# Second norm of the local layers on token rows between two turns, with a new order of the work

## The chip, the cores and the metric

One core of a Trainium2 chip (of eight) runs the whole program. The metric is the device time of one execution in microseconds (us). Engines: PE is TensorE (PEld its weight loads), DVE VectorE, ACT ScalarE, POOL GpSimd, SP SyncE, whose queue carries the transfers.

## The reference

x has the shape (8, 1024, 128), float32. Everything lies between two macaron halves and a causal attention of one head:

```python
x = x + 0.5 * local(layernorm(x))          # 2 layers of local attention and a gated second half
x = x + attention(layernorm(x), Wk, Wq, Wv)
x = x + 0.5 * local(layernorm(x))
# one layer of local(): 8 heads of 64, windows of 64 tokens that look one window back
h = shift_token(x); q, k, v = split(h @ wqkv)
q, k = rotary(l2norm(q) * qs, l2norm(k) * ks)
x = x + softmax(mask(8 * q @ k.T)) @ v @ wo
h = shift_token(x)
h = (h - mean(h)) / sqrt(var(h) + 1e-5) * ln_g + ln_b      # the second norm, over 128 features
a, g = split(h @ w1 + b1)                                  # 2 x 341
x = x + (a * gelu(g)) @ w2 + b2
```

## The kernel before, in words

x stays in SBUF as token rows. The state of a local layer, Y0, lies features on partitions and tokens along them, one row of 1026 columns per batch. 8192 tokens make 32 chunks of 256 (`NCH`). One chunk in one layer is a turn t: turns 0 to 63 are the two layers of the first half, 64 to 127 those of the second. Two turns are a pair u, for which the second half of the layer runs on 512 tokens. Layers 0 and 2 (the "even" ones) make their input from x by a first norm: `ln_stats`, `ln_root`, `ln_scale`, `ln_rows`, `turn_ln`, `y0_up`, `y0_down`. Layers 1 and 3 ("odd") turn their output back (`turn_y`) and add it to x (`x_next`).

A turn has two halves i of 128 tokens: `project` (three passes of fp32r, high and low parts), `square`, `sum_squares`, `rotate_cos`, `rotate_sin`, `rotate_add`, the twelve small steps of `root` (reciprocal root of the heads' norms by bit trick and three refinements), `normalise_qk`, `turn`, copies, `scores`, `row_max`, `exp_rows`, `row_inverse`, `scale_p`, `turn_p`, `copy_p`, `values`, `split_o`, `rest_of_o`, `wo`. A pair then has `y1_low` and `y1_high` (residual added, second token shift made), and the second norm. It runs with features on partitions: `split_yc` (ACT) and `rest_of_yc` (POOL) split Y1 into high and low fp32r parts NH and NL; `center` (PE, L656, L657) multiplies both by I - 1/128; `square_c` (ACT, L3680) squares; `var` (PE, L678) sums the squares over features by four products with a column of 1/128, tokens now on partitions; `add_eps` (DVE, L1955); `row_rstd` (POOL, L4725) takes the power -0.5; `turn_rstd` (PE, L686) spreads the four columns over all features by transposes; `copy_rstd` (ACT); `normalise` (DVE, L1963); `split_hn` (ACT) and `rest_of_hn` (POOL) split again. Then `to_gate`, `gelu`, `to_up`, `gate`, `down` (L710) and `y_next`.

Each engine follows a list of steps written out by hand: `first_steps`, `local(phase)` as a loop over rounds s (two turns and one pair per round, with fixed lags), `into_attention`, `attention`, `out_of_attention`, `last_steps`. Waits are on semaphores of the step's own inputs. PSUM has eight banks; `ROTA` and `FIRST_USERS` fix which steps use a bank in which order, and `vacant` lets a step wait until the bank's user before it has been read out:

```python
before = BEFORE[what, n]
if before:
    for done in emptied[before[0]]:
        on.wait_ge(done, emptied_at(*before))
```

Of the kernel before, what the change touches and what calls it, by code (L numbers as in the profile page):

```python
# [5335 lines left out]
```

## Time and profile before

| | |
|---|---|
| runs | 2748.17, 2749.38 (median), 2749.87 us |
| the profiled execution | 2748.73 us, of which its span 2746.9 us |
| PE busy | 2663.2 us (97%) |
| PEld busy | 2122.3 us (77%) |
| DVE busy | 2372.5 us (86%) |
| ACT busy | 2373.0 us (86%) |
| POOL busy | 2114.2 us (77%) |
| mean granted clock of TensorE | 0.993 |
| share of PE in the chain that ended last | 87% |

The span runs from the first to the last instruction; the rest of the time lies around it. Busy times are unions of an engine's instructions; PE's matmuls overlap, so that a share near 100% of the span can hold pipelining. "PS" is PSUM. A 128x128 fp32 matmul or 512-wide fp32 product counts as two instructions of the trace where it runs in two passes.

### The profile page before, as it was taken

To read this page: it belongs to the slowest core of one execution; us is meant where nothing else is said; L and a number is where in the kernel's file an instruction comes from. 1 tells how busy PE (TensorE), PEld (TensorE's weight loads), DVE (VectorE), ACT (ScalarE), POOL (GpSimd) and SP (SyncE) were. 2 spreads that over 40 slices of the span, in tenths; PEclk is the share of its full clock that TensorE was granted. 3 is DMA by queue.
4 is the path that set the end of the run, shared out by engine and by line. 5 is a ranking of instruction groups with operands and counts; after the bars stand their busy time and mean duration, and the time that the engine had idled before them with its cause. 6 is when DMAs were issued, how large, how long until landed. Compare 5 with 4: busy or idle time off the path is not lost.

```text
span 2746.9 us, 80395 instructions
## 1 busy us (share of the span) xinstructions
PE 2663.2 (97%) x29432; PEld 2122.3 (77%) x29432; DVE 2372.5 (86%) x6140; ACT 2373.0 (86%) x7281; POOL 2114.2 (77%) x2121
## 2 busy tenths in 40 slices
PE   5999999999999999999999999999999999999998
PEld 3777777778788888886777777787778788888886
DVE  7998999988888888896778999999998888888884
ACT  4998999999999999996443999999999999999995
POOL 6888888889888888882102988888889888888883
PEclk9999999999999999999999999999999999999998
DMA  3111111111111111110000111111111111111111
GB/s 96 46 44 30 27 38 23 31 27 34 31 23 31 31 37 28 31 23 12 8 1 3 35 27 29 30 33 31 23 31 30 30 31 34 36 38 31 38 31 32
DMA packets 63811, 83.96 MB, mean 31 GB/s; under 512 B 11539, under 2 KB 30653, under 8 KB 63421
## 3 DMA queue, kind: packets, MB, share of 16 engines
q1 hardware_dynamic: 63420, 78.82, 12.5%
q8 instruction: 238, 3.90, 0.6%
q14 instruction: 153, 1.25, 0.2%
HBM read 11.67 MB, written 4.19 MB: 6 GB/s over the span
## 4 chain that ended last, share of the span: by engine, by line
PE 87%; DVE 7%; issue 3%; ACT 1%; POOL 1%; DMA 0%; SPq 0%; POOLq 0%; DVEq 0%; ACTq 0%
PE PS L633 9%; PE PS L617 8%; PE PS L583 8%; PE PS L607 8%; PE PS L574 7%; PE PS L576 6%; PE PS L710 6%; PE PS L575 6%; PE PS L691 3%; PE PS L599 3%; PE PS L693 2%; PE PS L692 2%; PE PS L775 2%; PE PS L678 2%; PE PS L647 2%
## 5 line engine op out<-in xcount | busy, mean ns | idle before, releaser
L3652 ACT ACTIVATE P<-PS,MX 128x128 f32<-128x128 f32 x2048 | 735.2, 402 | 31.9 <-DVE MX L1912 31.0
L4714 POOL TENSOR_TENSOR P<-P,RI 128x512 f32<-128x512 f32 x512 | 532.0, 1043 | 226.3 <-DVE RI L1918 226.2
L4678 POOL TENSOR_TENSOR T<-T,SQ 128x512 f32<-128x512 f32 x512 | 654.5, 1287 | 55.7 <-DVE SQ L1877 32.8
L4691 POOL TENSOR_TENSOR T<-T,RN 128x512 f32<-128x512 f32 x512 | 527.8, 1048 | 33.2 <-DVE RN L1906 32.9
L3652 ACT ACTIVATION_READ_ACCUMULATOR P<-PS,MX 128x1 f32 x2048 | 489.9, 240 | 0.0
L574 PE MATMUL PS<-WH,YH 128*128 128x512 f32 x768 | 365.5, 476 | 30.1 <-DVE RV L1955 13.9
L3607 ACT ACTIVATE SQ<-PS 128x512 f32<-128x512 f32 x512 | 334.9, 656 | 63.9 <-PE PS L576 39.5
L1869 DVE TENSOR_TENSOR T<-PS,TAB 128x512 f32<-128x512 f32 x512 | 347.8, 681 | 37.4 <-ACT SQ L3607 35.1
L3659 ACT COPY PT<-PS 128x512 f32<-128x512 f32 x512 | 317.7, 631 | 52.3 <-PE PS L617 47.6
L1912 DVE TENSOR_REDUCE MX<-PS 128x4 f32<-128x512 f32 x512 | 347.4, 681 | 11.0 <-PE PS L607 6.5
L1877 DVE TENSOR_TENSOR SQ<-PS,TAB 128x512 f32<-128x512 f32 x512 | 348.4, 682 | 4.1
L1858 DVE TENSOR_REDUCE SS<-SQ 128x8 f32<-128x512 f32 x512 | 335.7, 674 | 5.2 <-ACT SQ L3607 4.2
L617 PE MATMUL PS<-CST,P 128*128 128x128 f32 x2048 | 313.9, 277 | 0.2 <-POOL P L4714 0.2
L633 PEld LDWEIGHTS PS<-PT,VP 128*64 128x64 f32 x8192 | 259.0, 138 | 65.2 <-issue 64.7
L576 PE MATMUL PS<-WH,YL 128*128 128x512 f32 x768 | 307.2, 400 | 0.0
L575 PE MATMUL PS<-WL,YH 128*128 128x512 f32 x768 | 305.4, 398 | 0.0
L583 PE MATMUL PS<-CST,T 128*128 128x128 f32 x2048 | 292.1, 276 | 6.6 <-POOL T L4691 4.0
L633 PE MATMUL PS<-PT,VP 128*64 128x64 f32 x8192 | 293.2, 225 | 1.3 <-ACT PT L3659 1.1
L583 PEld LDWEIGHTS PS<-CST,T 128*128 128x128 f32 x2048 | 237.0, 141 | 47.5 <-issue 18.1
L607 PE MATMUL PS<-KT,QT 64*64 64x128 f32 x8192 | 268.6, 270 | 0.0
L617 PEld LDWEIGHTS PS<-CST,P 128*128 128x128 f32 x2048 | 237.1, 141 | 31.1 <-issue 4.0
L607 PEld LDWEIGHTS PS<-KT,QT 64*64 64x64 f32 x8192 | 242.7, 133 | 17.9 <-issue 0.2
(135 smaller groups left out, 6085.5 us busy)
## 6 DMA issues: line engine op xcount, KB each, us to landing
VP<-VP SPq DMA_DIRECT2D x480, 128.0 KB, 2.3
out_dram<-X SPq DMA_DIRECT2D x16, 256.0 KB, 2.6
X<-in_L_attn_x_dram SPq DMA_DIRECT2D x7, 512.0 KB, 4.5
SG<-in_L_ffn_w_dram SPq DMA_DIRECT2D x5, 341.0 KB, 2.9
SG<-in_L_ffn_wqkv_dram SPq DMA_DIRECT2D x4, 384.0 KB, 3.4
SGQ<-in_L_ffn_wqkv_dram SPq DMA_DIRECT2D x4, 256.0 KB, 3.5
X<-in_table_dram SPq DMA_DIRECT2D x2, 512.0 KB, 6.1
P<-in_L_ffn_wo_dram SPq DMA_DIRECT2D x2, 256.0 KB, 3.1
```

The lines of the kernel that those rows point to most:

```text
L574: pe.matmul(PS[:, b, :], YH[:, k, :], WH[:, cols], start=True, stop=False)
L575: pe.matmul(PS[:, b, :], YH[:, k, :], WL[:, cols], start=False, stop=False)
L576: pe.matmul(PS[:, b, :], YL[:, k, :], WH[:, cols], start=False, stop=True).then_inc(projected[x], 1)
L583: ins = pe.transpose(PS[:, b, 128 * p:128 * p + 128], T1[:, k, 128 * p:128 * p + 128], ident)
L607: ins = pe.matmul(PS[64 * w:64 * w + 64, bank_of(f"S{2 * i + x}", t), 128 * p:128 * p + 128], QT2[at, s, p, m:m + WIN], KT[at, p, k:k + 12 ...
L617: ins = pe.transpose(PS[:, b, 128 * p:128 * p + 128], P[:, g, p, :], ident)
L633: ins = pe.matmul(PS[64 * x:64 * x + 64, b, 128 * p + m:128 * p + m + WIN], VP[:, s, 2 * i + w, d:d + 64], PT[:, 2 * i + x, p, m:m + WIN], ...
L1877: dve.tensor_tensor(SQ[:, (2 * n + 1 - x) % 3, :].rearrange("p (h t d) -> p h t d", h=HEADS, t=2), PS[:, b, :].rearrange("p (h t d) -> p h ...
L3652: ins = act.activation(P[:, g, p, :], PS[:, b, 128 * p:128 * p + 128], ACT.Exp, bias=MX[:, g, p:p + 1], accum_out=SM[:, g, p:p + 1])
L4678: pool.tensor_tensor(T1[:, k, :], T1[:, k, :], SQ[:, (2 * n + 1 - x) % 3, :], ALU.add).then_inc(added[x], 1)
L4691: pool.tensor_tensor(heads, heads, RN[:, t % 2, i, 8 * x:8 * x + 8].unsqueeze(2).broadcast_to([128, HEADS, DH]), ALU.mult).then_inc(scaled ...
L4714: pool.tensor_tensor(P[:, g], P[:, g], RI[:, g, :].unsqueeze(2).broadcast_to([128, NPAIR, 128]), ALU.mult).then_inc(p_scaled, 1)
```

## The change

The second norm goes over to token rows. `turn_rows` (PE) turns the four 128x128 blocks of Y1 into PSUM; `rows_stats` (DVE) takes mean and variance of each token by BN_STATS and BN_AGGR from there, adds eps and negates the means; `row_rstd` (POOL) takes the power and multiplies it with the negated means; `norm_rows` (ACT) applies scale and bias to the four blocks; `turn_back` (PE) turns them back; `split_hn` (ACT) reads PSUM, times ln_g, into NH, and `rest_of_hn` (DVE) forms NL. `center`, `var`, `turn_rstd`, `square_c`, `copy_rstd`, `add_eps`, `normalise`, `split_yc` and `rest_of_yc` go. The b1 products move from the variance bank into the bank of two `turn_ln` steps (turns 0 and 1), and the split of W1 (`round_w1`, `rest_of_w1`) becomes a step of its own. The lists of all engines and the users of all banks are new.

```diff
-OF_PAIRS = ("WO", "CE", "VA", "RS", "G0", "G1", "G2", "W2", "YT")
-ROUNDS = {0: (6, 32), 1: (38, 62)}
+OF_PAIRS = ("WO", "YR", "HB", "G0", "G1", "G2", "W2", "YT")
+ROUNDS = {0: (8, 32), 1: (40, 62)}
...
+    [("LT", 7), ("TK1", 9), ("YR", 6), ("P0", 9), ("HB", 6), ("P2", 9), ("LT", 6), ("G1", 6)],
...
-        def center(u):
...
-            pe.matmul(PS[:, b, :], CEN[:], NH[:], start=True, stop=False)
-            pe.matmul(PS[:, b, :], CEN[:], NL[:], start=False, stop=True).then_inc(center_mm, 1)
...
+        def turn_rows(u):
+            b, m = bank_of("YR", u), within(u)
+            on.wait_ge(y1_done, 2 * u + 2)
+            vacant(on, "YR", u)
+            for i in range(2 * TPC):
+                ins = pe.transpose(PS[:, b, 128 * i:128 * i + 128], Y1[:, m + 128 * i:m + 128 * i + 128], ident)
+            ins.then_inc(rows_turned, 1)
...
-            for i in range(2 * TPC):
-                ins = pe.matmul(PS[:, b, i:i + 1], SQL[:, 128 * i:128 * i + 128], ones, start=True, stop=True)
-            ins.then_inc(var_mm, 1)
...
-        def turn_rstd(u):
+        def turn_back(u):
+            b = bank_of("HB", u)
+            vacant(on, "HB", u)
+            on.wait_ge(rows_normed, u + 1)
             for i in range(2 * TPC):
+                ins = pe.transpose(PS[:, b, 128 * i:128 * i + 128], RN_ROWS[:, 128 * i:128 * i + 128], ident)
+            ins.then_inc(back_turned, 1)
...
+        def rows_stats(u):
+            b, n = bank_of("YR", u), 2 * TPC
+            done = (2 * n + 2) * u
+            on.wait_ge(rows_turned, u + 1)
+            on.wait_ge(rows_normed, u)
+            for i in range(n):
+                dve.bn_stats(RST[:, i, :], PS[:, b, 128 * i:128 * i + 128]).then_inc(row_stat, 1)
+            for i in range(n):
+                on.wait_ge(row_stat, done + i + 1)
+                dve.bn_aggr(RMV[:, i, :], RST[:, i, :]).then_inc(row_stat, 1)
+            on.wait_ge(row_stat, done + 2 * n)
+            dve.tensor_scalar(RMV[:, :, 1], RMV[:, :, 1], EPS, None, ALU.add).then_inc(row_stat, 1)
+            dve.tensor_scalar(RNM[:], RMV[:, :, 0], -1.0, None, ALU.mult).then_inc(row_stat, 1)
+
+        def rest_of_hn(u):
+            gamma = COLS[:, layer_of_pair(u) % 2, 6:7]
...
+            dve.scalar_tensor_tensor(NL[:], PS[:, bank_of("HB", u), :], gamma, NH[:].bitcast(F32), ALU.mult,
+                                     ALU.subtract).then_inc(hn_lo, 1)
...
+        def norm_rows(u):
+            b = bank_of("YR", u)
...
+            on.wait_ge(rstd, u + 1)
+            on.wait_ge(row_biased, u + 1)
+            for i in range(2 * TPC):
+                ins = act.activation(RN_ROWS[:, 128 * i:128 * i + 128], PS[:, b, 128 * i:128 * i + 128], ACT.Identity,
+                                     bias=RSB[:, 1, i:i + 1], scale=RSB[:, 0, i:i + 1])
+            ins.then_inc(rows_normed, 1)
...
+        def split_hn(u):
...
+            act.activation(NH[:], PS[:, bank_of("HB", u), :], ACT.Identity,
+                           scale=COLS[:, layer_of_pair(u) % 2, 6:7]).then_inc(hn_hi, 1)
...
         def row_rstd(u):
...
+            pool.tensor_tensor(RSB[:, 0, :], RMV[:, :, 1], NHALF[:], ALU.pow).then_inc(rstd, 1)
+            on.wait_ge(rstd, u + 1)
+            pool.tensor_tensor(RSB[:, 1, :], RSB[:, 0, :], RNM[:], ALU.mult).then_inc(row_biased, 1)
```

Where the steps stand now is shown at three places. First TensorE in a round of the kernel before, from the end of turn_p through centring (L656, L657), values (L633), scores (L599, L607) and the variance products (L678):

```order
L617 MATMUL PS<-CST,P 128x128 x4
L656 MATMUL PS<-NH,CEN 128x512
L657 MATMUL PS<-NL,CEN 128x512
L574 MATMUL PS<-WH,YH 128x512
L575 MATMUL PS<-WL,YH 128x512
L576 MATMUL PS<-WH,YL 128x512
L633 MATMUL PS<-PT,VP 64x64 x16
L599 MATMUL PS<-MLOC,IDB 64x512 x4
L607 MATMUL PS<-KT,QT 64x128 x16
L678 MATMUL PS<-CST,G 128x1 x4
```

Nothing but these and turn_rstd, a little later, belongs to the norm on TensorE. In the changed kernel the same engine, in an odd layer, has turn_rows (L682) ahead of both values (L659), turn_y (L746), projections (L600 to L602) and scores (L625, L633), up to the next turn_p (L643):

```order
L643 MATMUL PS<-CST,P 128x128 x4
L682 MATMUL PS<-CST,Y 128x128 x4
L659 MATMUL PS<-PT,VP 64x64 x32
L746 MATMUL PS<-CST,G 128x128 x4
L600 MATMUL PS<-WH,YH 128x512
L601 MATMUL PS<-WL,YH 128x512
L602 MATMUL PS<-WH,YL 128x512
L625 MATMUL PS<-MLOC,IDB 64x512 x4
L633 MATMUL PS<-KT,QT 64x128 x16
L600 MATMUL PS<-WH,YH 128x512
L601 MATMUL PS<-WL,YH 128x512
L602 MATMUL PS<-WH,YL 128x512
```

One more projection follows, then the turn_p that uses the bank of the turned rows again; turn_back (L699) comes after two more projections and two turns. On VectorE of the changed kernel the statistics (L2148 to L2154) stand between two steps of the root (L2095, L2097), behind a row maximum (L2105) and the last sine product of the turn (L2070):

```order
L2089 TENSOR_SCALAR PS<-PS 128x32
L2105 TENSOR_REDUCE MX<-PS 128x4
L2093 TENSOR_SCALAR RN<-PS 128x32
L2070 TENSOR_TENSOR SQ<-PS,TAB 128x512
L2095 SCALAR_TENSOR_TENSOR PS<-RN,PS 128x32
L2148 BN_STATS RST<-PS 128x6 x4
L2151 BN_AGGR RMV<-RST 128x2 x4
L2153 TENSOR_SCALAR RMV<-RMV 128x4
L2154 TENSOR_SCALAR RNM<-RMV 128x4
L2097 TENSOR_TENSOR PS<-PS,RN 128x32
```

In the kernel before, only add_eps stood in such a place, one small instruction; now ten do. GpSimd's next step behind the rotate_add of that sine product is row_rstd.

## Rows read from the trace of the kernel before

**Rows 1.** Stretches: us; busy of PE, PEld, DVE, ACT, POOL; PEclk, DMA share, GB/s

```profile
325.69:481.14 155.45, 152.43 (x1754) 121.11 (x1753) 142.97 (x383) 143.87 (x447) 132.33 (x135) 1.00 0.14 32
...
861.26:1011.74 150.48, 150.20 (x1754) 121.54 (x1753) 131.18 (x313) 141.11 (x440) 126.97 (x127) 1.00 0.14 33
```

**Rows 2.** Chain that ended last, its longest pieces: start us, us, what

```profile
286.84 2.58 PE PS L710 x6
...
598.02 2.58 PE PS L710 x6
673.25 2.58 PE PS L710 x6
...
1199.72 2.58 PE PS L710 x6
```

**Rows 3.** The same chain within one odd round

```profile
872.74 0.23 PE PS L656
...
873.91 1.08 PE PS L633 x32
874.99 0.34 PE PS L599 x4
875.33 0.87 PE PS L607 x32
876.20 0.98 PE PS L678 x8
...
878.97 0.44 PE PS L686 x4
```

**Rows 4.** Waits in four even rounds, 325.69 to 481.14: us in total, times, longest

```profile
DVE Y L1847 <- PE PS L720: 5.0, 4, 1.3
...
DVE Y L1987 <- PE PS L710: 4.4, 4, 1.1
```

**Rows 5.** VectorE in order of time, even round: start us, us, engine, line, operation

```profile
382.58 0.47 DVE L1799 BATCH_NORM_STATS2 ST<-X 128x6 f32<-128x128 f32 x2
382.97 0.30 DVE L1802 BATCH_NORM_AGGREGATE MV<-ST 128x2 f32<-128x6 f32 x2
383.30 0.74 DVE L1804 TENSOR_SCALAR MV<-MV 128x2 f32<-128x2 f32 x1
383.96 0.23 DVE L1918 RECIPROCAL RI<-SM 128x4 f32<-128x4 f32 x2
...
387.38 0.17 DVE L1804 TENSOR_SCALAR MV<-MV 128x2 f32<-128x2 f32 x1
387.46 0.18 DVE L1918 RECIPROCAL RI<-SM 128x4 f32<-128x4 f32 x1
```

**Rows 6.** GpSimd in order of time, the same stretch

```profile
381.97 2.05 POOL L4691 TENSOR_TENSOR T<-T,RN 128x512 f32<-128x512 f32 x2
...
387.72 1.04 POOL L4714 TENSOR_TENSOR P<-P,RI 128x512 f32<-128x512 f32 x1 [0.47 <-DVE RI L1918]
```

**Rows 7.** ScalarE in order of time, odd round

```profile
873.30 0.60 ACT L3680 ACTIVATE G<-PS 128x512 f32<-128x512 f32 x1
873.80 0.36 ACT L3652 ACTIVATE P<-PS,MX 128x128 f32<-128x128 f32 x1
874.05 0.20 ACT L3652 ACTIVATION_READ_ACCUMULATOR P<-PS,MX 128x1 f32 x1
874.14 0.37 ACT L3652 ACTIVATE P<-PS,MX 128x128 f32<-128x128 f32 x1
```

**Rows 8.** The chain that ended last, in the tail

```profile
2706.22 1.12 PE PS L686 x4
...
2725.86 1.01 POOL RV L4725
2726.87 3.94 issue
...
2732.16 0.80 PE PS L691
```

More of the change, by code:

```diff
@@ new lines, in local @@
+                project(t - 8, 0, Q)
+                down(s - 7)
+                turn(t - 9, 1, K)
+                project(t - 8, 1, K)
+                turn_p(t - 10, 0)
+                turn_p(t - 10, 1)
+                turn_p(t - 10, 2)
+                project(t - 8, 1, Q)
+                scores(t - 9, 0)
+                turn(t - 9, 1, Q)
+                turn_p(t - 10, 3)
+                turn_rows(s - 6)
+                values(t - 10, 0)
+                values(t - 10, 1)
+                turn_y(s - 7)
@@ new lines, in local @@
+                project(t - 8, 0, V)
+                scores(t - 9, 1)
+                project(t - 7, 0, Q)
+                project(t - 8, 1, V)
+                turn_p(t - 9, 0)
+                project(t - 7, 0, K)
+                project(t - 7, 1, K)
+                turn(t - 8, 0, Q)
+                turn(t - 8, 0, K)
+                turn_back(s - 6)
+                project(t - 7, 1, Q)
+                scores(t - 8, 0)
+                turn_p(t - 9, 1)
+                turn(t - 8, 1, K)
@@ new lines, in first_steps @@
+            rotate_sin(9, 0, K)
+            rotate_cos(9, 0, K)
+            ln_stats(10)
+            row_inverse(7, 3)
+            row_max(8, 0)
+            sum_squares(9, 1, K)
+            rest_of_hn(2)
+            rotate_cos(9, 1, K)
+            rotate_sin(9, 1, K)
+            row_inverse(8, 0)
+            row_max(8, 1)
+            sum_squares(9, 1, Q)
+            rotate_cos(9, 1, Q)
+            root(9, 0)
+            ln_scale(10)
+            root(9, 1)
+            ln_rows(10)
@@ new lines, in first_steps @@
+            root(9, 2)
+            rotate_sin(9, 1, Q)
+            root(9, 3)
+            row_inverse(8, 1)
+            root(9, 4)
+            y0_up(10)
+            root(9, 5)
+            rest_of_o(7, 0)
+            root(9, 6)
+            rest_of_o(7, 1)
+            root(9, 7)
+            ln_stats(11)
+            root(9, 8)
+            row_max(8, 2)
+            root(9, 9)
+            gate(2, 0)
+            gate(2, 1)
+            root(9, 10)
+            root(9, 11)
+            ln_scale(11)
@@ new lines, in first_steps @@
+            row_max(8, 3)
+            gate(2, 2)
+            ln_rows(11)
+            y1_low(3)
+            row_inverse(8, 2)
+            sum_squares(10, 0, K)
+            y0_up(11)
+            y1_high(3)
+            row_inverse(8, 3)
+            rotate_cos(10, 0, K)
+            rotate_sin(10, 0, K)
+            sum_squares(10, 0, Q)
+            rotate_cos(10, 0, Q)
+            rotate_sin(10, 0, Q)
+            y_next(2)
+            sum_squares(10, 1, K)
+            rotate_cos(10, 1, K)
@@ new lines, in first_steps @@
+            sum_squares(11, 1, K)
+            rest_of_hn(3)
+            rotate_cos(11, 1, K)
+            rotate_sin(11, 1, K)
+            row_inverse(10, 0)
+            row_max(10, 1)
+            sum_squares(11, 1, Q)
+            rotate_cos(11, 1, Q)
+            root(11, 0)
+            ln_scale(12)
+            root(11, 1)
+            ln_rows(12)
+            root(11, 2)
+            rotate_sin(11, 1, Q)
+            root(11, 3)
+            row_inverse(10, 1)
+            root(11, 4)
@@ new lines, in first_steps @@
+            y0_up(12)
+            root(11, 5)
+            rest_of_o(9, 0)
+            root(11, 6)
+            rest_of_o(9, 1)
+            root(11, 7)
+            ln_stats(13)
+            root(11, 8)
+            row_max(10, 2)
+            root(11, 9)
+            gate(3, 0)
+            gate(3, 1)
+            root(11, 10)
+            root(11, 11)
+            ln_scale(13)
+            row_max(10, 3)
+            gate(3, 2)
+            ln_rows(13)
+            y1_low(4)
+            row_inverse(10, 2)
@@ new lines, in first_steps @@
+            sum_squares(12, 0, K)
+            y0_up(13)
+            y1_high(4)
+            row_inverse(10, 3)
+            rotate_cos(12, 0, K)
+            rotate_sin(12, 0, K)
+            sum_squares(12, 0, Q)
+            rotate_cos(12, 0, Q)
+            rotate_sin(12, 0, Q)
+            y_next(3)
+            sum_squares(12, 1, K)
+            rotate_cos(12, 1, K)
+            rotate_sin(12, 1, K)
+            sum_squares(12, 1, Q)
+            row_max(11, 0)
+            root(12, 0)
+            rotate_cos(12, 1, Q)
@@ new lines, in first_steps @@
+            row_max(12, 1)
+            sum_squares(13, 1, Q)
+            rotate_cos(13, 1, Q)
+            root(13, 0)
+            ln_scale(14)
+            root(13, 1)
+            ln_rows(14)
+            root(13, 2)
+            rotate_sin(13, 1, Q)
+            root(13, 3)
+            row_inverse(12, 1)
+            root(13, 4)
+            y0_up(14)
+            root(13, 5)
+            rest_of_o(11, 0)
+            root(13, 6)
+            rest_of_o(11, 1)
+            root(13, 7)
+            ln_stats(15)
@@ new lines, in first_steps @@
+            root(13, 8)
+            row_max(12, 2)
+            root(13, 9)
+            gate(4, 0)
+            gate(4, 1)
+            root(13, 10)
+            root(13, 11)
+            ln_scale(15)
+            row_max(12, 3)
+            gate(4, 2)
+            ln_rows(15)
+            y1_low(5)
+            row_inverse(12, 2)
+            sum_squares(14, 0, K)
+            y0_up(15)
+            y1_high(5)
+            row_inverse(12, 3)
+            rotate_cos(14, 0, K)
+            rotate_sin(14, 0, K)
@@ new lines, in first_steps @@
+            sum_squares(14, 0, Q)
+            rotate_cos(14, 0, Q)
+            rotate_sin(14, 0, Q)
+            y_next(4)
+            sum_squares(14, 1, K)
+            rotate_cos(14, 1, K)
+            rotate_sin(14, 1, K)
+            sum_squares(14, 1, Q)
+            row_max(13, 0)
+            root(14, 0)
+            rotate_cos(14, 1, Q)
+            root(14, 1)
+            row_max(13, 1)
+            root(14, 2)
+            rotate_sin(14, 1, Q)
+            root(14, 3)
+            rows_stats(5)
```

4682 lines of the change are left out of this document (2623 added, 2059 removed), and 234 rows, old and new, of tables (FIRST_USERS, LAST_USERS, ROTA).

## Prediction

> **What bounds the kernel now.** I read the stretches of time first, then the chain of waits, then the waits by engine, then single rows of the engines. A round is two turns of the local layers with one second half (one pair); 64 pairs are worked off. The rows of the down projection (L710), one per round, give the period. In layers that make their input by a first norm (even layers) eight rounds take 598.02 - 286.84 = 311.2 us, 38.90 each; in those that turn their output back (odd layers) fourteen rounds take 1199.72 - 673.25 = 526.5 us, 37.60 each [rows 2]. The stretches say what limits them: in four odd rounds of 37.62 us TensorE is busy for 150.20 of 150.48 us, at full clock, while VectorE has 131.18, ScalarE 141.11 and GpSimd 126.97. In four even rounds of 38.86 us TensorE has 152.43 of 155.45, VectorE 142.97 [rows 1]. Odd rounds are TensorE's. Even rounds belong to nobody: VectorE stands twice per round for TensorE, 5.0 us at y0_up and 4.4 us at y_next in four rounds [rows 4], and TensorE comes late in turn. Without these waits (9.4 / 4 = 2.35) VectorE needs 38.86 - 2.35 = 36.5 us of an even round. In an odd one it has 131.18 / 4 = 32.8 busy; with the same small gaps between its own instructions (36.5 - 142.97 / 4 = 0.8) it needs 33.6.
>
> **TensorE, per pair.** A busy sum overstates pipelined matmuls, so prices come from the chain, where one follows another [rows 3]. Removed: centring, two passes of 0.23 as at L656 = 0.46; the variance products, 0.98; the four transposes that spread the root, 0.44. Sum 1.88. Added: turn_rows and turn_back, four transposes each, priced as the four of L686: 2 x 0.44 = 0.88. Net -1.00. All of it lies in the path of odd rounds: 37.60 - 1.00 = 36.6. Bounds: 0.2 more is saved if what follows the variance products no longer starts late; 0.3 less if the new transposes stand behind 64-row matmuls, as some of today's do.
>
> **VectorE, per pair.** The token-row statistics stand in rows that exist today for the first norm [rows 5]: BATCH_NORM_STATS2, two from 382.58 to 382.97, 0.195 each; BATCH_NORM_AGGREGATE, two to 383.30, 0.165 each; TENSOR_SCALAR 0.08 (387.38 to 387.46). rows_stats is 4 x 0.195 + 4 x 0.165 + 2 x 0.08 = 1.60. It loses add_eps (0.08, same kind). The 512-wide normalise becomes the 512-wide rest_of_hn, both with one PSUM and one SBUF operand: nothing. Net +1.5. Reading PSUM instead of SBUF is seen in no row for these operations; I take 0 and keep +0.1 each.
> The first TENSOR_SCALAR of the same round costs 0.66 (383.30 to 383.96), and it ends as GpSimd ends its run of two operations at 384.02 [rows 5, 6]; the one at 387.38 falls into a gap of GpSimd and costs 0.08. So each of the two new small operations may cost 0.08 or up to some 0.66. In the new order they stand where GpSimd's next instruction is row_rstd, which waits for them, so I take 0.08. The Trainium skill (SBUF — State Buffer, "two physically separate sides") says that a VectorE operation in a two-port mode and a GpSimd operation exclude each other for the whole instruction. By that rule both would be dear whenever GpSimd is busy, and the sum would be some 1.2 us per pair higher; the pair of rows above agrees with it.
> New need of VectorE: odd 33.6 + 1.5 = 35.1, under TensorE's 36.6: hidden, with 1.5 us of cover. Even 36.5 + 1.5 = 38.0, over TensorE's: so **even rounds become VectorE's, at 38.0** if the new order takes away the two standing waits of 2.35. It is built for that: y_next, today at once behind a gate and a row maximum, gets eight operations of about 0.6 behind the last gate; y0_up gets about one us behind ln_rows. I count nothing for the steps of the reciprocal root standing less often directly behind each other, and keep -0.5 for it.
>
> **ScalarE and GpSimd.** ScalarE loses four 512-wide passes of 0.50 (873.30 to 873.80) = 2.0 and gets four 128-wide ones of 0.25 (873.80 to 874.05) and one of 0.50 [rows 7]: -0.5, from 141.11 / 4 = 35.3, so it stays under 36.6. Table loads stay two per round, since the new passes stand among the exponentials' operations and the three gelus stand together. GpSimd loses two 512-wide subtractions of 1.0 or more each (two operations in 2.05, rows 6) and gets one 128x4 product, at most the 1.01 of the power beside it [rows 8]. It only gets more room.
>
> **Waits that are added.** Bank 3 now holds in turn turn_rows, turn_p(.,0), turn_back, turn_p(.,2). turn_p(.,0) must wait until ScalarE has emptied the turned rows. TensorE has between them two times values (1.08), turn_y (0.44), three projections of three passes as wide as centring's (3 x 0.23 = 0.70 each) and scores (0.34 + 0.87): 2.16 + 0.44 + 2.10 + 1.21 = 5.9 us [rows 3]. The way round is rows_stats 1.6, power 1.0, product 0.1 to 1.0, norm_rows 1.0, and four handovers of about 0.1: 4.1 to 5.0. That leaves 0.9 to 1.8 us for VectorE's lag behind TensorE at that point (four 512-wide operations stand between the last thing it must wait for and rows_stats). turn_back waits for ScalarE's copy of turn_p(.,0), behind which stand a square, one group of exponentials (four times 873.80 to 874.14, 1.4) and another square: again about level. I count 0, with +0.5 per round as the upper end. Queued behind a late turn_p are the projections and all that follow.
>
> **Ends.** The last pair has nothing to hide behind. Its chain from the power on holds 3.94 us of issue and starts the gate products only at 2732.16, the first of them 0.80 long [rows 8]. New: before the power a turn (0.44) and 1.6 in place of cast, subtraction, centring, square and variance (about 0.5 + 1.0 + 0.46 + 0.5 + 0.98 = 3.4), and behind it a product of up to 1.0, 1.0, 0.44, 0.5 and 0.66 (3.6) in place of 5.3: together 3 us less. The first rounds, and the crossing into and out of the middle attention, hold four more pairs at half the gain. Moving the b1 products into the bank of the first norm's turn, and the rounding of W1, happens two and four times in all: nothing. SP's queue keeps its transfers.
>
> **Sum.** Odd rounds 33 x 1.0 = 33; even rounds 27 x (38.90 - 38.0) = 24; four mixed pairs 4 x 0.5 = 2; end 3. Total 62 us from the profiled execution's own 2748.7 us: 2686.7. The median shown is 0.65 above that execution: **2687 us**, -2.3%.
>
> **Rivals.**
> - B, VectorE never binds: root steps interleave better (-0.5) and even rounds, too, run at TensorE's pace plus a little, 37.2. For: VectorE's gaps are latency. Against: 142.97 of 155.45 is busy already. Even gain 27 x 1.7 = 46: 2665 us.
> - C, VectorE binds more: one of the two small operations is held by GpSimd (+0.6), the statistics pay 4 x 0.1 for PSUM, so even rounds come to 39.0 and gain nothing; odd rounds stop at 36.8 through late handovers. Gain 33 x 0.8 + 3 = 29: 2720 us. For: GpSimd is busy 84% of an odd round.
> - D, the slower side: the loop through bank 3. If VectorE reaches rows_stats behind two further 512-wide operations and ScalarE reaches norm_rows behind a group of exponentials, the way round is 5.0 + 1.2 + 1.4 = 7.6 against 5.9 and turn_back repeats about as much: TensorE stands 2.5 us in each round. It decides from about 1.0 us per round; at 2.5 the balance is 60 x 1.5 = +90: 2840 us. For: the chain crosses four engines and has little slack. Against: ScalarE's and GpSimd's order put these steps just where they come due.
> - E, slow transposes. At the lower of TensorE's two levels (1.2 and 2.4 GHz) a group of four stands in the tail at 1.12 us, just after TensorE had been idle [rows 8]; in the full rounds, at a granted clock of 1.00, it takes 0.44 [rows 1, 3]. If transposes ran at the lower level here, the pair would lose 0.46 + 0.98 + 1.12 and get 2 x 1.12: only 0.32 gained, 33 x 0.32 + 24 + 5 = 40, so 2709 us. The Trainium skill (TensorE: Matmul & The Clock Gate, "PE-mode transpose") says that the full clock doesn't engage for transposes, at some 275 ns each. The trace, with 0.11 us each, speaks against it.
>
> **Chances.** Forecast 0.61, B 0.11, C 0.17, D 0.09, E 0.01, anything else, taken as faster, 0.01. A measurement of this kernel can tell about 0.2% (5.5 us) from no change. Of C's chance 0.02 and of D's 0.01 lie within that: same 0.03, slower 0.08, faster 0.89. The range reaches to C's 2720 and nearly to B's 2665, with a little for the ends: 2662 to 2721.
>
> **What would show it.** L710 spaced about 36.6 us in odd rounds with TensorE busy throughout; spaced about 38.0 in even rounds with no standing wait of VectorE at y0_up or y_next; rows_stats taking about 1.6 us from its first to its last instruction; no wait of TensorE for rows_normed or p_copied beyond some tenths. It is wrong if odd rounds stay over 37.2 (then a handover binds, and the waits name it), if even rounds come near 37 (B), or if the small TENSOR_SCALARs behind BATCH_NORM_AGGREGATE show 0.5 us and more (C).

## The result, and the profile after

The changed kernel takes **2705.93 us** (median of four, 2702.22 to 2707.76) against 2749.25 (median of four) of the kernel before on the same chip: ratio **0.984, 95% interval 0.982 to 0.986**. It is 43 us faster, 1.6%, where 62 were forecast; the time lies in the range, which reaches from 2662 to 2721. The profiled execution took 2702.22 us, its span is 2700.3; it is the fastest of the four, so what is read from it below adds up to 3 us more of gain than the medians show.

The page of the changed kernel, busy times and then the chain that ended last:

```profile
PE 2600.6 (96%) x29048; PEld 2060.3 (76%) x29048; DVE 2415.1 (89%) x6715; ACT 2321.4 (86%) x7345; POOL 1954.7 (72%) x2057
...
PE 46%; ACT 24%; DVE 19%; issue 6%; POOL 2%; ACTq 0%; DVEq 0%; POOLq 0%
```

TensorE's share of the chain was 87% before. Now the chain changes engines within every round. Four even rounds and four odd rounds, with the columns of [rows 1]:

```profile
301.67:452.41 150.74, 147.92 (x1731) 117.78 (x1732) 145.58 (x419) 139.81 (x451) 122.16 (x131) 1.00 0.14 32
...
876.61:1025.31 148.70, 147.21 (x1730) 117.89 (x1729) 133.63 (x349) 137.96 (x442) 116.80 (x123) 1.00 0.14 33
```

The chain's longest pieces give the periods, as [rows 2] did before: values (L659) in even rounds, the down projection (L723) in odd ones.

```profile
264.06 2.22 PE PS L659 x64
...
565.23 2.21 PE PS L659 x64
653.57 2.58 PE PS L723 x6
...
1174.01 2.58 PE PS L723 x6
```

Eight even rounds take 301.2 us, 37.65 each (38.90 before); fourteen odd ones take 520.4, **37.17** each (37.60 before). Forecast were 38.0 and 36.6.

Progress shows where the 46.6 us of span went. The third gate product of a pair on VectorE (L1975 before, L2169 after) ends, in us from the span's start:

| pair | before | after | ahead |
|---|---|---|---|
| 0 | 127.6 | 120.3 | 7.4 |
| 3 | 248.9 | 234.7 | 14.2 |
| 15 (last of the first even layer) | 711.2 | 688.0 | 23.2 |
| 31 (last odd one before the attention) | 1283.0 | 1252.8 | 30.2 |
| 32 (first behind it) | 1588.1 | 1560.1 | 28.1 |
| 47 | 2167.2 | 2125.7 | 41.5 |
| 63 | 2739.4 | 2692.8 | 46.6 |

So the start gives 14.2; even pairs 3 to 15 and 32 to 47 give 9.0 + 13.4 = 22.4; odd pairs with the end 7.0 + 5.1 = 12.1; the crossing takes back 2.1. The forecast was 24 for the even rounds, 33 + 3 for the odd ones and the end, 2 for start and crossing.

**The start.** VectorE of the kernel before (first fence) takes the statistics of three turns before the first normalised rows, and waits for x twice; the changed one (second fence) scales turn 0 as soon as the root is there. TensorE's first transposes begin at 16.66 us before and at 6.16 after. Not all of the 14.2 us is this: three even rounds lie in it, which gain about 1 us each anyway. And the same first steps don't give the same time each time: in the profiles of the variants of the changed kernel below, the third gate product of pair 0 ends between 119.5 and 124.3, a spread of 5 us, and this profile with 120.3 is near its lower end.

```profile
8.63 0.49 DVE L1799 BATCH_NORM_STATS2 ST<-X 128x6 f32<-128x128 f32 x2 [4.40 <-DMA X<-in_L_attn_x_dram]
...
14.90 0.49 DVE L1799 BATCH_NORM_STATS2 ST<-X 128x6 f32<-128x128 f32 x2 [5.36 <-DMA X<-in_L_attn_x_dram]
...
15.90 0.60 DVE L1827 SCALAR_TENSOR_TENSOR XN<-X,MV,PS 128x128 f32<-128x128 f32 x2
```

```profile
5.41 0.61 DVE L2017 SCALAR_TENSOR_TENSOR XN<-X,MV,PS 128x128 f32<-128x128 f32 x2
```

**The odd rounds.** The chain through one of them in the changed kernel:

```profile
882.68 0.87 PE PS L633 x32
883.55 0.60 PE PS L609 x4
884.18 0.59 ACT QT L4175
...
889.86 1.23 ACT G L4223 x3
...
897.30 0.52 ACT NH L4235
...
902.54 1.05 ACT P L4196 x5
903.60 0.14 issue
903.73 0.41 PE PS L625 x4
904.14 0.87 PE PS L633 x32
...
912.22 0.87 PE PS L609 x8
```

A loop of two parts. From the end of the turn of the queries (L609, 884.15) ScalarE works without a pause until the exponentials end at 903.6, and scores(.,1) (L625), which starts at 903.73, needs the bank that these exponentials empty: 19.6 us. Then TensorE works without a pause until the end of the next such turn: 17.6 us. norm_rows (L4223) and split_hn (L4235) both stand in ScalarE's part. Their prices, from ScalarE in order of time:

```profile
889.50 1.60 ACT L4223 ACTIVATE G<-PS,RSB 128x128 f32<-128x128 f32 x4
890.89 0.71 ACT L4151 ACTIVATE SQ<-PS 128x512 f32<-128x512 f32 x1
...
896.96 0.92 ACT L4235 ACTIVATE NH<-PS,COLS 128x512 fp32r<-128x512 f32 x1
897.71 0.43 ACT L4196 ACTIVATE P<-PS,MX 128x128 f32<-128x128 f32 x1
```

1.39 and 0.75 us, where 1.0 and 0.50 were forecast from [rows 7]. VectorE's and GpSimd's part of the norm in the same round:

```profile
886.50 0.89 DVE L2148 BATCH_NORM_STATS2 RST<-PS 128x6 f32<-128x128 f32 x4
887.30 0.37 DVE L2151 BATCH_NORM_AGGREGATE RMV<-RST 128x2 f32<-128x6 f32 x4
887.70 0.24 DVE L2153 TENSOR_SCALAR RMV<-RMV 128x4 f32<-128x4 f32 x1
887.85 0.16 DVE L2154 TENSOR_SCALAR RNM<-RMV 128x4 f32<-128x4 f32 x1
887.92 0.19 DVE L2097 TENSOR_TENSOR PS<-PS,RN 128x32 f32<-128x32 f32 x1
```

```profile
888.09 1.02 POOL L5443 TENSOR_TENSOR RSB<-RMV,NHALF 128x4 f32<-128x4 f32 x1 [0.18 <-DVE RNM L2154]
889.19 0.20 POOL L5445 TENSOR_TENSOR RSB<-RSB,RNM 128x4 f32<-128x4 f32 x1
```

rows_stats takes 1.42 us (1.6 forecast) and the two small TENSOR_SCALARs 0.15 and 0.07 up to the next start. The first of them is held all the same, though only for its last 0.07 us. GpSimd was in the middle of a product:

```profile
886.64 1.28 POOL L5400 TENSOR_TENSOR T<-T,SQ 128x512 f32<-128x512 f32 x1 [1.63 <-DVE SQ L2070]
```

It ends at 887.92, and L2153 at 887.94. GpSimd was in an operation when L2153 started in 58 of the 64 pairs, and in each of them L2153 ended 0.02 to 0.03 us behind that operation; with GpSimd idle it lasts 0.17 (0.24 here, 0.98 in the one long case). On the other side norm_rows has hardly any room: GpSimd's product with the means ends at 889.39, and norm_rows starts at 889.50.

**The even rounds.** The chain here:

```profile
309.19 0.75 DVE G L2169
...
324.69 0.80 DVE RST L2148 x4
325.49 0.29 DVE RMV L2151 x4
325.81 0.24 DVE RMV L2153
326.19 1.03 POOL RSB L5443
327.29 0.21 POOL RSB L5445
...
327.97 1.16 ACT G L4223 x3
329.12 0.14 issue
329.26 0.63 PE PS L643 x4
```

From the gates to rows_stats VectorE works almost without a pause (15.5 us); the norm then passes GpSimd and ScalarE to turn_p (L643), and TensorE carries the rest. VectorE's standing waits at y0_up and y_next [rows 4] are gone.

### The profile page after: what moved, and what is told of

Its sections match the earlier page's. It is cut to its first block, busy times and chain, and to the rows that moved or that the text cites. A ratio compares the mean times of both kernels' runs of the same rounds, so it can differ in the third digit from the quotient of the medians.

```text
span 2700.3 us, 80117 instructions
## 1 busy us (share of the span) xinstructions
PE 2600.6 (96%) x29048; PEld 2060.3 (76%) x29048; DVE 2415.1 (89%) x6715; ACT 2321.4 (86%) x7345; POOL 1954.7 (72%) x2057
## 4 chain that ended last, share of the span: by engine, by line
PE 46%; ACT 24%; DVE 19%; issue 6%; POOL 2%; ACTq 0%; DVEq 0%; POOLq 0%
ACT P L4196 11%; PE PS L609 4%; PE PS L633 4%; PE PS L643 4%; PE PS L723 3%; PE PS L704 3%; ACT PT L4203 3%; ACT G L4223 3%; DVE SS L2051 3%; PE PS L706 3%; PE PS L705 3%; PE PS L600 3%; DVE SQ L2070 3%; PE PS L602 2%; DVE MX L2105 2%
## 5 line engine op out<-in xcount | busy, mean ns | idle before, releaser
L4196 ACT ACTIVATE P<-PS,MX 128x128 f32<-128x128 f32 x2048 | 751.6, 432 | 5.2 <-DVE MX L2105 4.3
L4196 ACT ACTIVATION_READ_ACCUMULATOR P<-PS,MX 128x1 f32 x2048 | 546.8, 271 | 0.0
L600 PE MATMUL PS<-WH,YH 128*128 128x512 f32 x768 | 348.2, 453 | 19.6 <-POOL YL L5389 9.2
L2051 DVE TENSOR_REDUCE SS<-SQ 128x8 f32<-128x512 f32 x512 | 345.8, 676 | 16.4 <-ACT SQ L4151 14.4
L2105 DVE TENSOR_REDUCE MX<-PS 128x4 f32<-128x512 f32 x512 | 345.4, 677 | 8.9 <-PE PS L633 8.5
L2070 DVE TENSOR_TENSOR SQ<-PS,TAB 128x512 f32<-128x512 f32 x512 | 348.1, 681 | 0.4
L643 PE MATMUL PS<-CST,P 128*128 128x128 f32 x2048 | 293.2, 276 | 23.0 <-ACT G L4223 15.1
L4203 ACT COPY PT<-PS 128x512 f32<-128x512 f32 x512 | 301.8, 647 | 4.8 <-PE PS L643 4.6
L602 PE MATMUL PS<-WH,YL 128*128 128x512 f32 x768 | 305.7, 398 | 0.0
L609 PE MATMUL PS<-CST,T 128*128 128x128 f32 x2048 | 296.4, 275 | 8.4 <-ACT P L4196 5.8
L609 PEld LDWEIGHTS PS<-CST,T 128*128 128x128 f32 x2048 | 238.7, 141 | 71.8 <-issue 47.5
L659 PEld LDWEIGHTS PS<-PT,VP 128*64 128x64 f32 x8192 | 255.8, 138 | 41.8 <-issue 37.2
L643 PEld LDWEIGHTS PS<-CST,P 128*128 128x128 f32 x2048 | 228.0, 141 | 70.9 <-issue 34.5
L659 PE MATMUL PS<-PT,VP 128*64 128x64 f32 x8192 | 278.6, 224 | 2.5 <-ACT QT L4175 2.4
L633 PE MATMUL PS<-KT,QT 64*64 64x128 f32 x8192 | 269.7, 270 | 0.0
L633 PEld LDWEIGHTS PS<-KT,QT 64*64 64x64 f32 x8192 | 244.1, 134 | 17.6 <-issue 0.4
```

The lines of the kernel that those rows point to most:

```text
L600: pe.matmul(PS[:, b, :], YH[:, k, :], WH[:, cols], start=True, stop=False)
L609: ins = pe.transpose(PS[:, b, 128 * p:128 * p + 128], T1[:, k, 128 * p:128 * p + 128], ident)
L633: ins = pe.matmul(PS[64 * w:64 * w + 64, bank_of(f"S{2 * i + x}", t), 128 * p:128 * p + 128], QT2[at, s, p, m:m + WIN], KT[at, p, k:k + 12 ...
L643: ins = pe.transpose(PS[:, b, 128 * p:128 * p + 128], P[:, g, p, :], ident)
L659: ins = pe.matmul(PS[64 * x:64 * x + 64, b, 128 * p + m:128 * p + m + WIN], VP[:, s, 2 * i + w, d:d + 64], PT[:, 2 * i + x, p, m:m + WIN], ...
L2051: dve.tensor_reduce(SS[:, t % 2, i, 8 * x:8 * x + 8], SQ[:, (2 * n + 1 - x) % 3, :].rearrange("p (h d) -> p h d", h=HEADS), AX.X, ALU.add) ...
```

## Experiments

Four of the kernels leave out part of the statistics (norm_one_pass, stats_one_block, one_block_one_pass, both_cuts_rows_twice); the others compute everything. All runs are compared by the period of a round: the distance between the ends of the third gate product of two pairs, divided by the rounds between. Even: pairs 3 to 12 and 36 to 44; odd: pairs 16 to 28 and 48 to 60.

| run | time, us | ratio to before, 95% | even | odd |
|---|---|---|---|---|
| before | 2749.25 | | 38.89, 38.87 | 37.62, 37.55 |
| changed | 2705.93 | 0.982 to 0.986 | 37.82, 37.61 | 37.17, 37.28 |
| norm_one_pass | 2679.21 | 0.974 to 0.976 | 37.64, 37.42 | 36.75, 36.86 |
| rows_turned_twice | 2706.09 | 0.983 to 0.986 | 37.81, 37.59 | 37.17, 37.31 |
| square_late | 2871.92 | 1.044 to 1.047 | 41.31, 40.93 | 40.64, 40.32 |
| scores_late | 2743.02 | 0.998 to 0.999 | 38.95, 38.74 | 37.60, 37.62 |
| before_rstd_twice | 2772.95 | 1.008 to 1.010 | 39.22, 39.22 | 38.07, 38.00 |
| turn_p_late | 2702.82 | 0.982 to 0.985 | 37.81, 37.60 | 37.18, 37.28 |
| stats_twice | 2746.21 | 0.998 to 1.000 | 38.50, 38.32 | 37.80, 37.87 |
| norm_on_dve_odd | 2732.48 | 0.993 to 0.995 | 37.82, 37.64 | 38.03, 38.19 |
| stats_one_block | 2701.44 | 0.981 to 0.984 | 37.65, 37.45 | 37.18, 37.26 |
| one_block_one_pass | 2669.80 | 0.970 to 0.973 | 37.38, 37.21 | 36.65, 36.74 |
| half_norm_on_dve | 2721.85 | 0.989 to 0.993 | 37.81, 37.60 | 37.47, 37.85 |
| both_cuts_rows_twice | 2684.82 | 0.976 to 0.979 | 37.38, 37.20 | 37.08, 37.17 |

**norm_one_pass**

```diff
-            for i in range(2 * TPC):
-                ins = act.activation(RN_ROWS[:, 128 * i:128 * i + 128], PS[:, b, 128 * i:128 * i + 128], ACT.Identity,
-                                     bias=RSB[:, 1, i:i + 1], scale=RSB[:, 0, i:i + 1])
+            act.activation(RN_ROWS, PS[:, b, :], ACT.Identity, bias=RSB[:, 1, 0:1], scale=RSB[:, 0, 0:1])
```

> norm_rows becomes one 512-wide activation with the scale and bias of the first block; the statistics of the other three blocks' tokens are left out of the normalised rows. On ScalarE it takes about 0.50 us in place of 1.39. Theory S (odd rounds are bound by a loop of two parts: ScalarE without a pause from the turn of the queries of the odd turn's second half to the exponentials that free the bank of scores(.,1), 19.6 us, then TensorE from these scores to that turn, 17.6 us): odd rounds fall from 37.17 by 0.6 to 0.9 us, stopped by TensorE at about 36.4; even rounds, whose TensorE waits 0.5 us for the normalised rows before turn_p(.,0), fall by 0.3 to 0.6. Time 2706 - 33 x 0.7 - 27 x 0.45 = 2671 us. Theory P (TensorE is still what bounds odd rounds): odd rounds keep 37.1 to 37.2, only even ones gain, 2694 us. Theory V (VectorE binds both): 2706 us.

ScalarE in order of time:

```profile
919.13 0.87 ACT L4222 ACTIVATE G<-PS,RSB 128x512 f32<-128x512 f32 x1
920.09 0.60 ACT L4151 ACTIVATE SQ<-PS 128x512 f32<-128x512 f32 x1
```

One pass lasts 0.87, more than assumed. The square behind it starts 0.96 after it, and 0.09 of that is a wait for the products that it reads. The chain of the same round:

```profile
919.82 0.25 PE PS L602
920.09 0.60 ACT SQ L4151
...
932.93 0.41 PE PS L625 x4
```

So 1.39 - 0.96 = 0.43 us leave the loop, and odd rounds fall by 0.42. The time of an odd round of the changed kernel hangs on ScalarE's part, although ScalarE is busy for only 137.96 of 148.70 us. The limit of the gain is seen too: in this kernel the loop goes over TensorE, from the turn of the queries (913.17) to these products (920.07), and enters ScalarE's list only at the square. In even rounds the pass takes 0.68 to the next start (326.16 to 326.84) against 1.38, and of these 0.70 us only 0.18 show.

**rows_turned_twice**

```diff
-            for i in range(2 * TPC):
+            for i in (0, 1, 2, 3, 0, 1, 2, 3):
                 ins = pe.transpose(PS[:, b, 128 * i:128 * i + 128], Y1[:, m + 128 * i:m + 128 * i + 128], ident)
```

> turn_rows issues its four transposes twice: 0.44 us more on TensorE per pair, which stands inside ScalarE's part of the loop. Theory S: odd rounds rise by no more than 0.2 us (TensorE had about 0.3 of waiting there); even rounds, in which turn_rows is part of the way through bank 3, rise by 0.2 to 0.44. Time 2706 + 3 to 6 + 5 to 12 = 2715 to 2724 us. Theory P: odd rounds rise by 0.44 in full and even ones too, 2706 + 60 x 0.44 = 2732 us.

Nothing, in either kind of round: TensorE's own work is not what bounds the changed kernel at this place, and in even rounds rows_stats does not wait for turn_rows, against what theory S expected there. Theory P falls. The dose just fits: by norm_one_pass TensorE's products are ready some 0.43 us before the square of the changed kernel starts.

**square_late**

```diff
-                square(t - 3, 1, Q)
                 copy_p(t - 5, 2)
                 copy_p(t - 5, 3)
                 copy_q(t - 4, 1)
                 exp_rows(t - 4, 1)
+                square(t - 3, 1, Q)
```

> On ScalarE square(t - 3, 1, Q) moves from before copy_p(t - 5, 2) to behind exp_rows(t - 4, 1); nothing else changes. Theory S: one 512-wide pass of about 0.55 us leaves the continuous part of ScalarE, so odd rounds fall by 0.4 to 0.55, to 36.6 to 36.8 us; even rounds, whose VectorE gets these squares later and has little room, change by -0.1 to +0.3. Time 2706 - 33 x 0.48 + 27 x 0.1 = 2693 us, between 2687 and 2701. Theory P: odd rounds unchanged, 2706 us; theory V: unchanged or up to 0.5 per round slower, since sum_squares gets its input later, 2706 to 2735 us.

A clear miss: 3.0 to 3.5 us more per round, 166 in all. The waits of the window 900 to 1060 name it:

```profile
PE PS L625 <- DVE SQ L2070: 11.5, 4, 2.9
DVE SS L2051 <- ACT SQ L4151: 11.4, 4, 2.8
```

scores(.,1) uses two banks. One is emptied by the exponentials, the other held the queries Q1 of the turn behind it and is emptied by VectorE's sine product (L2070), which follows from this square. I had looked only at the first. In the changed kernel the two are ready within half a us of each other (the sine product ends at 903.20, the exponentials at 903.60), so the square is as critical as the exponentials it was moved behind. The wait of 2.9 us per round is most of the loss; the granted clock of TensorE is also lower here, 0.96 in this window against 1.00 in the changed kernel, and no run separates its share.

**scores_late**

```diff
-                scores(t - 8, 1)
                 to_gate(s - 6, 1)
                 to_gate(s - 6, 2)
+                scores(t - 8, 1)
```

> On TensorE scores(t - 8, 1) moves behind to_gate(s - 6, 1) and to_gate(s - 6, 2). Theory S: two groups of products of about 0.7 us each leave TensorE's part of the loop and fill its wait for ScalarE, so odd rounds fall until TensorE itself binds, by 0.5 to 0.75 us to 36.4 to 36.7; even rounds change by 0 to -0.2, or the later scores cost 0.2. Time 2706 - 33 x 0.6 = 2686 us, between 2680 and 2695. Theory P: 2706 us, or slower by the later row maxima.

Slower, by 0.4 in odd and 1.1 in even rounds: the third gate uses the bank of values(.,0), which rest_of_o empties behind split_o, and that stands behind the same exponentials. TensorE then waited at the gate, with the scores queued behind it:

```profile
925.82 0.46 PE L704 MATMUL PS<-NH,W1H 128*85 128x512 f32 x1 [0.47 <-DVE OTL L2115]
```

Both reorderings that the loop theory recommended failed at a bank's other user. They say nothing against the loop, and much about how it is tied.

**before_rstd_twice**

```diff
-            for i in range(2 * TPC):
+            for i in (0, 1, 2, 3, 0, 1, 2, 3):
                 ins = pe.transpose(PS[:, b, 128 * i:128 * i + 128], RV[:, 1, i:i + 1].broadcast_to([128, 128]), ident)
```

> In the kernel before, turn_rstd issues its four transposes twice: 0.44 us more on TensorE per pair. If TensorE bound odd rounds there (37.60), they rise by 0.44 in full; even rounds, in which nobody was always busy, by 0.2 to 0.44. Time 2748 + 33 x 0.44 + 27 x 0.3 = 2771 us. The same dose cost the changed kernel nothing in either kind of round. If odd rounds rise by under 0.2, TensorE was not their bound before either, and the step of the prediction was wrong already there; 2748 to 2756 us.

Odd rounds rise by 0.45 for 0.44 us of transposes: they were TensorE's before the change. The same dose costs nothing after it. Even rounds rise by 0.33.

**turn_p_late**

```diff
-                turn_p(t - 9, 0)
                 project(t - 7, 0, K)
+                turn_p(t - 9, 0)
```

> On TensorE turn_p(t - 9, 0) moves behind project(t - 7, 0, K), so that 0.70 us of products fill its wait for the normalised rows. Even rounds (37.6 to 37.8) then fall until VectorE's unbroken run from the last gate to rest_of_hn and the transposes behind it bind, by about as much as norm_one_pass gained there, 0.18, at most 0.5. Odd rounds, bound by ScalarE's part of the loop, in which copy_p(t - 5, 0) stands well behind, are unchanged within 0.05. Time 2706 - 27 x 0.18 = 2701 us, between 2693 and 2706. If TensorE's own sum were the bound: unchanged.

Unchanged to 0.01 in both kinds of round. The 0.5 us that TensorE waits for the normalised rows in even rounds is not itself the bound: with turn_p late, the copy of its result and turn_back behind it come later by as much (the chain then passes ScalarE's copy and reaches TensorE at turn_back).

**stats_twice**

```diff
+            for i in range(n):
+                dve.bn_stats(RST[:, n + i, :], PS[:, b, 128 * i:128 * i + 128])
             for i in range(n):
                 dve.bn_stats(RST[:, i, :], PS[:, b, 128 * i:128 * i + 128]).then_inc(row_stat, 1)
```

> rows_stats issues its four BATCH_NORM_STATS2 twice: about 0.8 us more on VectorE per pair (0.20 each). If VectorE's run is what holds even rounds, they rise by 0.7 to 0.8. In odd rounds VectorE waits 1.5 us for the products of the gates and some 0.9 us for exponentials, so they rise by 0 to 0.2, unless the rotation of Q1, which frees the bank of scores(.,1) at nearly the same time as the exponentials do, comes later: then by up to 0.8. Time 2706 + 27 x 0.75 + 33 x 0.1 = 2730 us, up to 2750.

Even rounds +0.70, as expected. Odd rounds **+0.61**, where 0 to 0.2 were expected, or more by a later rotation of Q1: VectorE waits over 2 us in an odd round, yet work added to it comes out at three quarters of its size. The chain of this kernel in odd rounds goes from the statistics over GpSimd's power to norm_rows, which had 0.1 us of room and now waits (in four rounds, 876 to 1025):

```profile
ACT G L4225 <- POOL RSB L5447: 2.2, 4, 0.5
```

**norm_on_dve_odd**: norm_odd is VectorE's, called behind rest_of_o(t - 2, 0); in odd layers ScalarE's norm_rows does nothing.

```diff
+        def norm_odd(u):
...
+            for i in range(2 * TPC):
+                ins = dve.tensor_scalar(RN_ROWS[:, 128 * i:128 * i + 128], PS[:, b, 128 * i:128 * i + 128],
+                                        RNM[:, i:i + 1], RSB[:, 0, i:i + 1], ALU.add, ALU.mult)
```

> In odd layers VectorE normalises the rows: four TENSOR_SCALAR with two per-token operands (add the negated mean, times the reciprocal root), 128 wide each, behind rest_of_o(t - 2, 0), in place of ScalarE's four activations; even layers stay as they are. ScalarE's part of the loop is 1.39 us shorter, and VectorE gets 4 x 0.2 = 0.8 us in rounds in which it waits over 2 us. norm_one_pass, with 0.89 less on ScalarE, gave 0.42 per odd round; if ScalarE's part is the bound, this gives 0.3 to 0.5 as well: 2706 - 32 x 0.4 = 2693 us, between 2689 and 2700. If VectorE's rotation of Q1 is as close to binding as ScalarE, nothing or a loss of up to 0.4: up to 2719 us.

Odd rounds +0.9. The chain of this kernel in an odd round shows the way it takes:

```profile
932.64 1.35 DVE G L2165 x4
934.34 0.60 DVE MX L2105
935.22 0.88 ACT P L4216 x5
```

The four TENSOR_SCALARs take 0.34 each (1.35 for four), not 0.2, and stand ahead of a row maximum (L2105) for which ScalarE's exponentials now wait (ACT P L4216 <- DVE MX L2105, 5.1 us in four rounds). VectorE's run from the sums of squares on is the other way into ScalarE's part of the loop.

**stats_one_block**

```diff
+            n = 1
             for i in range(n):
                 dve.bn_stats(RST[:, i, :], PS[:, b, 128 * i:128 * i + 128]).then_inc(row_stat, 1)
```

> rows_stats takes the statistics of the first block alone (one BATCH_NORM_STATS2, one BATCH_NORM_AGGREGATE), and all four blocks are normalised with them; the other three blocks' statistics are left out. VectorE has about 3 x 0.20 + 3 x 0.07 = 0.8 us less per pair, ScalarE and TensorE the same work. stats_twice, with 0.8 more, cost 0.70 per even round and 0.63 per odd one. Theory W (in even rounds VectorE's path binds alone; in odd rounds it ends together with ScalarE's): even rounds fall by 0.3 to 0.7, odd rounds by no more than 0.2, since ScalarE's part holds them at 37.0 to 37.2. Time 2706 - 27 x 0.5 - 33 x 0.1 = 2689 us, between 2680 and 2698. If VectorE alone is the bound of odd rounds too, they fall by 0.6: 2706 - 27 x 0.6 - 33 x 0.6 = 2670 us.

Even rounds fall by 0.16 only, not 0.3 to 0.7, odd rounds not at all. VectorE binds upwards, not downwards: something else is ready at nearly the same time in both kinds.

**one_block_one_pass**: the edits of the last run and of norm_one_pass together.

> Both cuts together: statistics of the first block alone (0.8 us less on VectorE) and one 512-wide activation with its scale and bias (0.9 less on ScalarE); left out as in the two runs with one of them. Theory W: each cut alone leaves the other engine's path, so both together give more in odd rounds than the sum of the two, down to where TensorE itself binds, which the prediction put at 36.6 from the trace of before: 36.4 to 36.6, 0.6 to 0.8 less. Even rounds fall by 0.5 to 0.9 to about 37.0. Time 2706 - 33 x 0.65 - 27 x 0.7 = 2666 us, between 2658 and 2674. If odd rounds stay above 36.8, TensorE, or a third path, holds them, and the two engines are not the cause.

Odd rounds 36.65, 0.52 less than in the changed kernel, where the two cuts alone gave 0 and 0.42; even rounds 0.42 less, where they alone gave 0.17 and 0.18. In both kinds together gives a little more than the sum, as for two paths that end close to each other. The chain of an odd round is that of norm_one_pass: TensorE to the products of the square, ScalarE to the exponentials, TensorE from scores(.,1) on.

```profile
915.94 0.25 PE PS L602
...
916.71 1.38 ACT P L4197 x7
...
928.96 0.41 PE PS L625 x4
```

**half_norm_on_dve**: in odd layers these are VectorE's, behind row_max(t - 3, 2); ScalarE does blocks 0 and 1.

```diff
+            for i in (TPC, TPC + 1):
+                ins = dve.tensor_scalar(RN_ROWS[:, 128 * i:128 * i + 128], PS[:, b, 128 * i:128 * i + 128],
+                                        RNM[:, i:i + 1], RSB[:, 0, i:i + 1], ALU.add, ALU.mult)
```

> Whole computation. In odd layers ScalarE normalises the first two blocks only, and VectorE the other two (two TENSOR_SCALAR, 0.34 us each as measured in norm_on_dve_odd, after ScalarE's part is done) behind row_max(t - 3, 2), that is behind the maximum on which ScalarE's next exponentials wait, not before it. ScalarE's part of the odd loop is 0.70 us shorter; VectorE's 0.68 us more stands where it next waits 0.9 us for exponentials. Theory W with its places: odd rounds fall by 0.25 to 0.4 (norm_one_pass took 0.89 off ScalarE and gave 0.42), even rounds are unchanged: 2706 - 32 x 0.33 = 2695 us, between 2692 and 2700. If VectorE's total counts and not the place, odd rounds rise by 0.3 to 0.5: 2716 to 2722 us.

Another miss, +0.3 to +0.6 in odd rounds. Behind the row maximum the rows come too late for turn_p:

```profile
933.35 0.63 PE L643 MATMUL PS<-CST,P 128*128 128x128 f32 x4 [0.67 <-DVE G L2168]
```

So this is the loop through bank 3 of rival D, which the changed order keeps just out of reach: its place between the row maximum and turn_p has no room on VectorE.

**both_cuts_rows_twice**: one_block_one_pass with rows_turned_twice.

> one_block_one_pass (odd rounds 36.65, even 37.38), with turn_rows issuing its four transposes twice: 0.44 us more on TensorE per pair. In the changed kernel this dose cost nothing in either kind of round. If TensorE is the bound of odd rounds once ScalarE and VectorE are relieved, as the prediction's 36.6 supposes, they rise by 0.3 to 0.44: 2670 + 33 x 0.4 + 27 x 0.1 = 2686 us, between 2680 and 2696. If ScalarE's part still binds at 36.65, nothing: 2670 us, up to 2674.

Odd rounds +0.43 for 0.44 us of transposes: turn_rows stands in TensorE's part of the loop now, and the two cuts have used up its room. That TensorE alone is the bound at 36.65 is not shown, since 12.6 us of ScalarE are still in the chain (916.2 to 928.8) and TensorE waits 0.25 us for the exponentials in each round. Without this wait it would need some 36.4 (an estimate: 36.65 less 0.25). Even rounds stay at 37.38, so these are still not TensorE's.

No version tried beats the changed kernel with the whole computation; turn_p_late is level with it. That the start's gain comes from the order of VectorE's first steps was read from the traces and not tried by itself. Nor does any run keep the old order with the new norm: how much of the loop in odd rounds is the norm's and how much the order's is open.

## Why the prediction was right or wrong

- **Direction, range:** right. Faster was given 0.89, and 2705.93 lies inside 2662 to 2721. It is nearest to rival E's 2709 in time, but not by E's mechanism. That the total came as near as 19 us is partly luck: the odd rounds with the end gave 12 us of the 36 forecast, and start and crossing gave 12 where 2 were forecast.
- **TensorE's net of -1.00 per pair: right, as far as it can be seen.** Odd rounds were TensorE's before (a dose of 0.44 costs 0.45). With the other engines relieved they run at 36.65 (forecast 36.6); TensorE alone would need some 36.4 by the estimate above, which is the prediction's own lower bound of 0.2. Transposes ran at full speed: the four of turn_rows stand in the chain of norm_one_pass at 0.44 us, at a granted clock of 1.00, which settles E. The Trainium skill's figure that the prediction weighed there (TensorE: Matmul & The Clock Gate, "PE-mode transpose", some 275 ns each) was set against the wrong number. It agrees with how long one lasts (272 ns on average at L682, 277 at L617 before), but they overlap, and 0.11 us is the distance from one to the next. That the full clock doesn't engage is not seen in these rounds, where transposes stand between other products; transposes alone were not run.
- **"So it stays under 36.6", of ScalarE in odd rounds: this is the step that failed.** It costs 33 x (37.2 - 36.6) = some 20 us, more than the whole miss of 62 - 46.6 = 15 in the profiled executions; start and crossing gave 10 of it back. It failed twice. The size: norm_rows and split_hn take 1.39 + 0.75 and not 1.0 + 0.5, so that the norm's balance on ScalarE is -2.0 + 2.14 = +0.1, not -0.5 (with everything else that ScalarE does, its busy time in four odd rounds fell, from 141.11 to 137.96). And the kind of argument: I set a sum of busy time (35.3 less 0.5) against a period of 36.6. What counts is the part of ScalarE's list that lies between a TensorE step and a bank that TensorE needs back, 19.6 us without a pause, plus TensorE's 17.6 us around it. The new order puts both norm steps into that part. norm_one_pass shows it (0.43 taken out of the loop, 0.42 gained). With both steps as short as forecast the part would be 0.64 shorter and the loop 36.5, an estimate from these rows. So the mis-sized term alone is as large as the miss of 0.57 per round, and the sum of busy time could not show that it counts.
- **VectorE "hidden, with 1.5 us of cover" in odd rounds: wrong.** The cover is below 0.2: stats_twice costs 0.61 of 0.8. The reason is the same kind: VectorE's waits are at the gates and behind the exponentials, while what counts at rows_stats is that GpSimd's product is ready only 0.1 us before norm_rows starts.
- **Even rounds "become VectorE's, at 38.0": nearly right.** 37.82 and 37.61 were measured, 0.2 to 0.4 better; rows_stats is 0.2 cheaper than forecast, its aggregates 0.1 each rather than 0.165. But VectorE does not bind alone: 0.8 more costs 0.70, about 0.75 less gives 0.17.
- **The two small TENSOR_SCALARs at 0.08, not 0.66: right in size** (0.15 and 0.07), **but by luck.** The reason given was that GpSimd's next instruction waits for them; in fact GpSimd was still in the 512-wide product before it, and held the first of them as rival C feared. It had only 0.2 us left to run. Rival C's condition holds, its price does not; its other half (odd rounds above 36.6 "through late handovers") is what happened, and 37.2 is worse than C's 36.8.
- **Waits added "count 0": right in size.** turn_p waits 0.5 us per even round for the normalised rows, but turn_p_late shows that this is no bound. D did not come, and half_norm_on_dve shows how near it is.
- **Start and end: wrong.** The first rounds gave 14.2 us, not one or two. The list of VectorE's first steps was in front of me, three statistics ahead of the first rows in the old one; I priced the norm there and did not compare when the first transposes can start. From pair 61 to 63 the gain is 1.3, not 3.

## What to carry to other kernels

- Cover is not a busy share. Before an engine's room is counted, follow its list from the step of another engine that starts a run to the buffer that this run gives back; if the run has no pause, a step put into it costs its full length, however idle the engine is elsewhere, as long as no other path into the same run ends later.
- When a change takes work off the one bound of a well-balanced schedule, look for two runners-up: cutting either alone gave 0 and 0.42 us here, both together 0.52, and adding to VectorE cost three quarters of the dose. A dose on each engine (the same instructions issued twice) tells quickly which runs bind and how much room the others have. It tells it of the place where it stands: a dose that costs its full size shows that this piece is in the loop, not that its engine is the whole of the bound.
- Where a change rewrites the order, compare also the first instructions of each engine: nearly a third of this gain (14.2 of 46.6 us) came from the first four pairs.
